# A fused attention and state-space kernel: its channel stage laid out with time on the rows and four channels a product

## The reference, cut to what matters

```python
x1  = x + attention(x)                  # out = o @ Wo.T + bo, o[b, c, 128]
y   = causal_conv(x1 * mask, taps[c])   # plus D[c] * x1, times mask again
W   = (unpacked_6_bit(qweight) - zero_point[n]) * scale[n]
out = x1 + y @ W.T + bias               # over time, for each b and c
```

## Time and profile before

| | us |
|---|---|
| median of 3 runs | 744.96 |
| lowest, highest | 742.61, 747.47 |
| the profiled execution, its own time | 743.27 |
| its span in the profile | 741.5 |
| busy: TensorE matmul, VectorE, ScalarE, GpSimd | 720.1, 610.1, 390.3, 215.9 |

### The profile page before, as it was taken

One profiled execution on the slowest core, in us unless ns is written; L12 is line 12 of the kernel. 1 busy time (PEld: TensorE's weight loads), 2 busy tenths in 40 slices (PEclk: granted clock), 3 DMA queues, 4 the chain that ended last, 5 costly groups with the idle time before them and its releaser, 6 DMA issues.

```text
span 741.5 us, 18118 instructions
## 1 busy us (share of the span) xinstructions
PE 720.1 (97%) x7540; PEld 595.0 (80%) x7540; DVE 610.1 (82%) x1085; ACT 390.3 (53%) x736; POOL 215.9 (29%) x224
## 2 busy tenths in 40 slices
PE   8999999999999999999999999999988899999996
PEld 6866878786978778697869787786766799999996
DVE  4878989998997977697767769777987688888887
ACT  4686475565656765746656565657552322333221
POOL 5370110030002011530300000000221778877772
PEclk9999999999999999999999999999999999999999
DMA  7800100020001001000200100022024288988861
GB/s 229 308 3 2 58 5 1 2 61 3 1 17 46 2 2 57 2 4 13 62 2 1 29 31 3 2 61 61 26 75 136 72 185 200 216 191 203 204 133 72
DMA packets 37108, 51.52 MB, mean 69 GB/s; under 512 B 7427, under 2 KB 23203, under 8 KB 36899
## 3 DMA queue, kind: packets, MB, share of 16 engines
q1 hardware_dynamic: 35042, 49.77, 25.7%
q0 software_dynamic: 1024, 0.53, 0.3%
q10 hardware_dynamic: 960, 0.06, 0.1%
HBM read 41.71 MB, written 8.63 MB: 68 GB/s over the span
## 4 chain that ended last, share of the span: by engine, by line
PE 88%; DVE 6%; ACT 2%; DMA 1%; issue 1%; SPq 0%; POOL 0%; DVEq 0%
PE ps L724 34%; PE ps L773 7%; PE ps L616 6%; PE ps L618 6%; PE ps L617 6%; PE ps L796 4%; PE ps L1052 4%; PE ps L1053 4%; PE ps L665 3%; PE ps L624 2%; PE ps L626 2%; PE ps L625 2%; PE ps L1021 2%; PE ps L1009 1%; PE ps L1011 1%
## 5 line engine op out<-in xcount | busy, mean ns | idle before, releaser
L1153 ACT ACTIVATE qt<-ps,m_bias 128x512 f32<-128x512 f32 x228 | 145.8, 685 | 89.3 <-PE ps L724 89.3
L724 PE MATMUL ps<-q_high,m_high 64*128 64x512 f32 x768 | 165.0, 397 | 0.0
L724 PE MATMUL ps<-q_high,m_low 64*128 64x512 f32 x768 | 161.3, 387 | 0.0
L724 PE MATMUL ps<-q_low,m_high 64*128 64x512 f32 x768 | 113.7, 387 | 0.0
L724 PEld LDWEIGHTS ps<-q_high,m_high 64*128 64x128 f32 x768 | 88.7, 184 | 14.8 <-issue 5.1
L724 PEld LDWEIGHTS ps<-q_high,m_low 64*128 64x128 f32 x768 | 88.8, 184 | 9.2
L1425 DVE TENSOR_TENSOR z_low<-ps,z_high 128x512 fp32r<-128x512 f32 x128 | 79.8, 683 | 19.7 <-ACT z_high L1173 19.7
L724 PEld LDWEIGHTS ps<-q_low,m_high 64*128 64x128 f32 x768 | 81.1, 184 | 10.2
L1173 ACT CAST z_high<-ps 128x512 fp32r<-128x512 f32 x128 | 66.7, 597 | 18.3 <-PE ps L840 9.2
L508 POOL TENSOR_TENSOR o_sum<-o_part,o_part 128x512 f32<-128x512 f32 x7 | 9.1, 1302 | 229.3 <-ACT o_part L1183 229.3
L1347 ACT COPY x1T_far<-ps 128x128 f32<-128x128 f32 x32 | 8.5, 265 | 103.8 <-PE ps L1021 103.8
(11 more groups left out here) (269 smaller groups left out, 1660.1 us busy)
## 6 DMA issues: line engine op xcount, KB each, us to landing
x_raw<-in_x_groups SPq DMA_DIRECT2D x32, 256.0 KB, 4.2
x_s<-in_x SPq DMA_DIRECT2D x32, 256.0 KB, 5.7
out<-res SPq DMA_DIRECT2D x31, 256.0 KB, 3.4
toep_high<-taps_scratch SPq DMA_DIRECT2D x32, 192.0 KB, 4.4
toep_low<-taps_scratch SPq DMA_DIRECT2D x32, 192.0 KB, 5.0
w_raw<-in_w_groups SPq DMA_DIRECT2D x8, 512.0 KB, 7.6
toep_far<-taps_scratch SPq DMA_DIRECT2D x32, 64.0 KB, 5.6
rope_raw<-in_rope_rows SPq DMA_DIRECT2D x8, 192.0 KB, 7.5
```

The costliest lines, as they stand in the source:

```text
L724: mm = pe.matmul(ps[:, fold_bank(u, j) + e, :], weights[rows, (GH * g + j) // 2, c, :], moving[c][rows, :], start=start, stop=stop)
L1153: act.activation(qt[:, j, :], ps[:, fold_bank(u, j) + j % 2, :], ACT.Identity, bias=m_bias[:, h:h + 1]).then_inc(s["qt_done"], 1)
```

## The change

The channel stage now has time on the rows throughout, and works on groups g of four channels.

- `attention_out(g, tt)` gives 128 times of four channels and 128 sequences (512 columns), with `Wo` stationary; five of them (`AHEAD`) are issued ahead of the first convolution. VectorE's `x1_made` adds `bo` (a column) and `x` in one instruction; ScalarE and VectorE split the result (`x1_rounded`, `x1_rest`). No transposes.
- `convolved(c)` reads one channel of the group's tiles. `through_ffn(g, n)` has the weights `wfT` stationary and makes 128 output times for the four channels, in 8 matmuls of 512 columns, one such product in each round.
- The sum of `y` over time is made by VectorE (`y_pair`), GpSimd (`y_sum`) and two matmuls with ones per group (`total`). ScalarE turns it into the correction with bias (`rest`), GpSimd adds `x1`, and VectorE scales the product and adds in one instruction.
- The weights come laid out by the host (`ffn_words`, `woT`, `x_channels`, the output likewise). `turned_ffn` and `turned_wo` are gone. VectorE masks bits in 4 instructions, ScalarE floats, GpSimd subtracts the zero row into `wfT` and makes `mask`, both during units 14 and 15. `woT_high` is made in unit 14 by ScalarE, `woT_low` ahead of `begun_last(0)` by VectorE, which also waits for `wfT` there. Five one-column VectorE instructions for the bit masks are new at the kernel's start.
- SP loads `x` in pieces of 1 MB per group, two before the stage; of the Toeplitz tiles only two channels' are issued at `t_ready` GH * NU, the other four behind `out_done`.

The diff, cut to its core: most removed lines are left out, since they stand in the listing above.

```diff
+    qw = t("qw", [P, TT, T], I32, at=wcT_at)
+    q_float = t("q_float", [P, TT, T], at=wcT_at)
...
+    wfT = t("wfT", [P, TT, T], F32R, at=m_at)
...
+    x_t = [t(f"x_t{n}", [P, TT, 4, B], at=at) for n, at in enumerate((m_at + 24 * KB, sc_at, qt_at, qt_at + 8 * KB))]
...
-    sp.wait_ge(s["feat_ready"], 4 * NS)
...
-        sp.dma_start(x_s[c][:], d["x"][:, c, :]).then_inc(ring_x[c], 16)
...
+    sp.dma_start(cols[:], d["columns"]).then_inc(s["cols_in"], 16)
+    sp.dma_start(z_row[:], d["zero_row"].partition_broadcast(P)).then_inc(s["row_in"], 16)
+    sp.dma_start(woT_raw[:], d["woT"]).then_inc(s["wo_in"], 16)
+    def load_x1(g):
+        sp.dma_start(x_t[g % RX][:], d["x_channels"][g]).then_inc(ring_x[g % RX], 16)
...
+    def store(i):
+        sp.wait_ge(s["res_done"], i + 1)
+        sp.dma_start(out[i // 4, :, i % 4], rest[i % RW][:]).then_inc(stored[i % RW], 16)
+    sp.wait_ge(s["t_ready"], GH * LAST)
+    load_x1(0)
+    sp.wait_ge(s["turn_done"], 4 * LAST)
+    load_x1(1)
+    sp.wait_ge(s["t_ready"], GH * NU)
+    sp.wait_ge(s["taps_stored"], 96)
+    for c in range(2):
         load_toep(c)
...
-            load_x1(c + RX - R)
...
+    sp.wait_ge(s["out_done"], NU)
+    for c in range(2, R):
         load_toep(c)
...
+    load_x1(2)
+    for c in range(C + 6):
+        if c == 4:
+            load_x1(3)
         if c + R < C:
...
+            sp.wait_ge(s["conv_ready"], c + 1)
+            load_toep(c + R)
+        if 0 <= c - 6:
+            store(c - 6)
+        if c >= 8 and c % 4 == 0 and c // 4 + 2 < NG:
+            sp.wait_ge(s["rest_ended"], c - 4)
+            load_x1(c // 4 + 2)
...
+    pool.wait_ge(s["row_in"], 16)
+    chain(pool.tensor_scalar(z_row[:], z_row[:], 0.0, 63.0, ALU.max, ALU.min))
+    chain(pool.tensor_scalar(z_row[:], z_row[:], MAGIC, None, ALU.add))
+    chain(pool.tensor_scalar(z_row[:], z_row[:], MAGIC, None, ALU.subtract))
+    pool.wait_ge(s["len_in"], 16)
+    chain(pool.tensor_copy(len_f[:], len_i[:]))
+    for k in range(TT):
+        pool.tensor_scalar(mask[:, k, :], len_f[:], l_pos[:, 0:1], float(P * k), ALU.subtract,
+                           ALU.is_gt).then_inc(s["mask_ready"], 1)
+        pool.wait_ge(s["mask_ready"], k + 1)
     pool.wait_ge(s["t_ready"], GH * LAST)
...
-    pool.tensor_tensor(c_row[:], c_row[:], s_row[:], ALU.mult).then_inc(s["c_done"], 1)
+    for k in range(TT):
+        pool.wait_ge(s["wf_ready"], k + 1)
+        pool.tensor_tensor(wfT[:, k, :], q_float[:, k, :], z_row[:], ALU.subtract).then_inc(s["wfT_done"], 1)
+        pool.wait_ge(s["wfT_done"], k + 1)
+    front(LAST - 1)
+    pool.memset(f(ones_r[:]), 1.0).then_inc(s["ones_ready"], 1)
...
-    def with_bo(c):
...
+    for c in range(C + 5):
+        i = c - 5
+        if i >= 0:
+            g, n = i // 4, i % 4
+            pool.wait_ge(s["rest_begun"], i + 1)
+            pool.tensor_tensor(rest[i % RW][:], rest[i % RW][:], x_t[g % RX][:, n], ALU.add).then_inc(s["rest_ended"], 1)
+        if c < C:
+            g, ch = c // 4, c % 4
+            pool.wait_ge(s["yh_done"], c + 1)
+            if g >= 2 and ch == 0:
+                pool.wait_ge(s["f_ready"], 4 * (g - 1))
+            pool.tensor_tensor(y_low[g % 2][:, :, ch, :], y[c % 2][:], f(y_high[g % 2][:, :, ch, :]),
+                               ALU.subtract).then_inc(s["yl_done"], 1)
+            pool.wait_ge(s["y_paired"], c + 1)
+            if g >= 1 and ch == 0:
+                pool.wait_ge(s["sum_low_done"], g)
+            pool.tensor_tensor(y_sum[:, ch, :], y_pair[c % 2][:, 0, :], y_pair[c % 2][:, 1, :],
+                               ALU.add).then_inc(s["y_summed"], 1)
...
-    def turned_ffn(k):
...
-            mm = pe.transpose(ps[:, FFN_BANK[k], n * P:(n + 1) * P], wf[n][:, k * P:(k + 1) * P], ident[:])
...
-    turned_wo()
...
-    pe.wait_ge(s["woT_done"], 1)
     kept_busy(BX, 4)
...
+    def attention_out(g, tt):
+        i = 4 * g + tt
+        if tt == 0:
+            pe.wait_ge(s["ol_done"], g + 1)
+        if i == 0:
             pe.wait_ge(s["ol_early"], 1)
...
             pe.wait_ge(s["woT_done"], 1)
             pe.wait_ge(s["zl_done"], 8 * NU)
...
-    def turned(c):
...
             pe.wait_ge(s["s_taken"], 4 * NU)
...
+        if i >= AHEAD:
+            pe.wait_ge(s["x1_done"], i - 1 if i >= AHEAD + 2 else i - AHEAD + 1)
+        part = slice(tt * P, (tt + 1) * P)
+        three(ps[:, a_bank(i), :], woT_high[:, part], woT_low[:, part], run_of(o_high[g % 2][:]),
+              run_of(o_low[g % 2][:])).then_inc(s["a_ready"], 1)
     def convolved(c):
...
+        g, ch, q = c // 4, c % 4, c % 2
+        if ch == 0:
+            pe.wait_ge(s["x1_low_done"], 4 * g + 4)
         pe.wait_ge(ring_toep[c % R], 48 * (c // R + 1))
         if c >= 2:
             pe.wait_ge(s["y_done"], c - 1)
         for e in range(TT - 1):
             rows = slice(e * P, (e + 1) * P)
...
+            three(ps[:, 4 + q, e * P:T].rearrange("p (t b) -> p t b", b=B), toep_high[c % R][:, rows],
+                  toep_low[c % R][:, rows], x1_high[g % 2][:, 0:TT - e, ch, :], x1_low[g % 2][:, 0:TT - e, ch, :],
+                  e == 0, False)
+        pe.matmul(ps[:, 4 + q, (TT - 1) * P:T], toep_far[c % R][:], x_t[g % RX][:, 0, ch, :], start=False,
+                  stop=True).then_inc(s["conv_ready"], 1)
+    def total(g):
+        pe.wait_ge(s["sum_low_done"], g + 1)
+        if g == 0:
+            pe.wait_ge(s["o_last"], 2)
+            pe.wait_ge(s["ones_ready"], 1)
         else:
...
+            pe.wait_ge(s["rest_begun"], 4 * g)
+        pe.matmul(ps[:, TOTAL_BANK, :], ones_r[:], run_of(sum_high[:]), start=True, stop=False)
+        pe.matmul(ps[:, TOTAL_BANK, :], ones_r[:], run_of(sum_low[:]), start=False, stop=True).then_inc(s["total_ready"], 1)
+    def through_ffn(g, n):
+        i = 4 * g + n
+        if n == 0:
+            pe.wait_ge(s["yh_done"], 4 * g + 4)
+        if i == 0:
+            pe.wait_ge(s["wfT_done"], TT)
+        if i < 3:
+            pe.wait_ge(s["x1_done"], i + 3)
+        else:
+            pe.wait_ge(s["res_done"], i - 2)
         for k in range(TT):
...
+            pe.matmul(ps[:, F_BANK[i % 3], :], wfT[:, k, n * P:(n + 1) * P], run_of(y_high[g % 2][:, k]), start=(k == 0),
+                      stop=False)
+        if n == 0:
+            pe.wait_ge(s["yl_done"], 4 * g + 4)
+        for k in range(TT):
+            mm = pe.matmul(ps[:, F_BANK[i % 3], :], wfT[:, k, n * P:(n + 1) * P], run_of(y_low[g % 2][:, k]), start=False,
+                           stop=(k == TT - 1))
         mm.then_inc(s["f_ready"], 1)
-    def projected_last():
...
+    for i in range(AHEAD):
+        attention_out(i // 4, i % 4)
+    for c in range(C):
+        g, ch = c // 4, c % 4
+        if c + AHEAD < C:
+            attention_out((c + AHEAD) // 4, (c + AHEAD) % 4)
+        if g >= 1 and ch == 1:
+            total(g - 1)
+        convolved(c)
+        if g >= 1:
+            through_ffn(g - 1, ch)
+    through_ffn(NG - 1, 0)
+    total(NG - 1)
+    for n in range(1, 4):
+        through_ffn(NG - 1, n)
...
+    def x1_rounded(i):
+        g, tt = i // 4, i % 4
+        act.wait_ge(s["x1_done"], i + 1)
+        if g >= 2 and tt == 0:
+            act.wait_ge(s["conv_ready"], 4 * (g - 1))
+        act.copy(x1_high[g % 2][:, tt], x_t[g % RX][:, tt]).then_inc(s["x1_high_done"], 1)
+    for i in range(TT):
+        x1_rounded(i)
+    split(1)
+    x1_rounded(TT)
+    for c in range(C + 5):
+        g, ch, i = c // 4, c % 4, c - 5
+        if ch == 0 and 1 <= g <= NG:
+            act.wait_ge(s["y_summed"], 4 * g)
+            if g >= 2:
+                act.wait_ge(s["total_ready"], g - 1)
+            act.copy(sum_high[:], y_sum[:]).then_inc(s["sum_high_done"], 1)
+        if ch == 1 and 2 <= g + 2 < NG:
+            split(g + 2)
+        if i >= 0:
+            act.wait_ge(s["total_ready"], i // 4 + 1)
+            act.wait_ge(s["z_scaled"], 1)
+            if i >= RW:
+                act.wait_ge(stored[i % RW], 16 * (i // RW))
+            act.activation(run_of(rest[i % RW][:]), ps[:, TOTAL_BANK, :], ACT.Identity, bias=fb_c[:, i % 4:i % 4 + 1],
+                           scale=z_scale[:, i % 4:i % 4 + 1]).then_inc(s["rest_begun"], 1)
+        if c + AHEAD < C:
+            x1_rounded(c + AHEAD)
+        if c < C:
+            act.wait_ge(s["y_done"], c + 1)
+            if g >= 2 and ch == 0:
+                act.wait_ge(s["f_ready"], 4 * (g - 1))
+            act.copy(y_high[g % 2][:, :, ch, :], y[c % 2][:]).then_inc(s["yh_done"], 1)
...
+    dve.wait_ge(s["woT_high_done"], 1)
+    dve.tensor_tensor(woT_low[:], woT_raw[:], f(woT_high[:]), ALU.subtract).then_inc(s["woT_done"], 1)
     begun_last(0)
...
+    def x1_made(i):
+        g, tt = i // 4, i % 4
+        dve.wait_ge(s["a_ready"], i + 1)
+        if tt == 0:
+            dve.wait_ge(ring_x[g % RX], 16 * (g // RX + 1))
+        if i == 0:
+            dve.wait_ge(s["cols_in"], 16)
+        x1 = run_of(x_t[g % RX][:, tt])
```

(42 more changed lines are left out.)

383 lines of the change are left out of this document (78 added, 305 removed).

## The result

The changed kernel takes 740.67 us (median of 9 runs, 738.13 to 742.93). The kernel before, run beside it, takes 744.96 (9 runs, 742.05 to 747.60). The ratio is 0.9943, with a 95% interval of 0.9921 to 0.9965: faster by 0.6%, or 4.3 us, where 10.0 was forecast. That lies within 1%, and inside the range. The sign was right, the size less than half of what was forecast. The profiled execution took 739.18 us, with a span of 737.3 us instead of 741.5, where 731.5 was forecast.

A forecast was written before the change was run, and what follows sets the result against it. TensorE was taken as the bound, VectorE and transfers not far behind. 714.5 to conv(31)'s end, 15.6 behind it and 1.2 for the clock gave 731.3; span taken as 731.5 (10.0 less), median 735.0, range 729.5 to 742.

The forecast's parts named there:

- first attention product: End of the attention: TensorE's first attention product of the channel stage at 572.1, 4.15 us earlier; bounds 0 and -4.4.
- conv(0) to the end of conv(31): Channel stage: convolutions, 26 attention and 27 linear products, `total` and 1.3 of waits sum to 133.4, ending at 714.5.
- Does something hide under that?: Channel stage: VectorE 3.6, GpSimd 3.0 and ScalarE below 2.5 fit in TensorE's mean round of 4.56; no transfer cost.
- Pause: End of the attention: TensorE's 3.22 us "issue" stop at 558.31, blamed on full transfer queues, goes; first attention product 4.15 earlier.
- pause stays: Rival, chance 0.15: the 3.22 us stop before the channel stage remains, 4.15 us are lost, time 739.2.
- Fill and clock: Start of the channel stage: TensorE idles 4.6 us, conv(0) starts at 581.1, lower clock adds 1.2 (ends 0 and +3.3).
- Steady rounds, plain ones: Channel stage: period of 4.45 without `total`, 0.46 more every fourth round, mean 4.56 instead of 4.86; strided operands cost 0.
- Tail: Behind conv(31): GpSimd's last four adds end at 11.3, then VectorE 0.755 and a store of 3.4: 15.6.
- The loop is not TensorE's: Rival, chance 0.09: VectorE or GpSimd waits for another engine each round, period stays 4.86, 8.4 us lost, time 743.4.
- Slower by repeated late instructions: Rival, chance 0.11: bunched 1 MB loads repeatedly delay TensorE's instruction blocks in the channel stage; 754.4 with four stops.

The follow-up runs named there:

- b2: b1 with GpSimd's `rest` in the round with `total` also waiting for `sum_low`; 734.91 us, 0.9884 of the kernel before.
- a1: Changed kernel with TensorE's `total` issued behind its round's convolution instead of ahead of it; 732.57 us, 0.9828 of the kernel before.
- b1: Changed kernel with GpSimd's `y_low` of a group's first channel waiting until VectorE's `sum_low` has ended; 737.04 us, 0.9889 of the kernel before.
- h1: Changed kernel with `total` behind the convolution, ScalarE's `split(1)` early, and VectorE's part of `split(1)` moved to GpSimd; 728.18 us, 0.9780 of the kernel before.
- e1: Kernel before with only two channels' Toeplitz tiles loaded ahead of `out_done`, the other four and the x rows behind it; 741.95 us, 0.9957 of the kernel before.
- d1: Changed kernel with all six channels' Toeplitz tiles loaded ahead of `out_done`, as in the kernel before; 740.53 us, 0.9942 of the kernel before.
- g1: d1 with 11 small float32 products, 22 matmuls whose results are overwritten, added ahead of `values(14,0)`; 744.23 us, 1.0010 of the kernel before.
- c1: Changed kernel with `split(1)` early: ahead of ScalarE's x1 roundings, behind VectorE's second `x1_made`; 738.23 us, 0.9901 of the kernel before.

## Why the prediction was right in sign and wrong in size

By its own steps, in the profiled execution:

| step | forecast | measured |
|---|---|---|
| first attention product | 572.1 | 573.32 |
| from there to conv(0), clock included | 10.2 | 9.45 |
| conv(0) to the end of conv(31) | 133.4 | 139.3 |
| behind conv(31) | 15.6 | 15.2 |
| span | 731.3 | 737.3 |

*The step that failed* is the one under "Does something hide under that?": "VectorE per round: ... a fourth each of split and `sum_low` 0.34: 3.6 of 4.56", and with it "the first `total` waits for VectorE's `sum_low` (+0.2). From then on VectorE waits for TensorE." It priced VectorE's new SBUF-to-SBUF instructions by rows in which GpSimd did not hold them up, and laid GpSimd's 3.0 us a round beside them as if the two had nothing in common. In the rounds with `total` two of them were stretched by 1.91 us in all. Of the seven totals ahead of conv(31) the first did not wait, and six waited 7.1 in all: +6.9 against the forecast's 0.2. `total` with its neighbours took 0.71 in those instead of 0.46: +1.5. conv(0) ran at the lower clock, 2.20 instead of 1.81, which the forecast had in another term: +0.4. Against that a plain round is shorter than forecast. By the starts from 650.31 to 654.65 it is 0.69 + 1.57 + 0.14 + 1.94 = 4.34: the plain-float32 tail takes 0.14 where 0.22 was read in the kernel before, and the linear layer 1.94 where 1.84 and 0.11 were forecast: 31 rounds, -3.4. Together +5.4 of the 5.9 between 133.4 and 139.3. The other 0.5 is not taken apart in full. Part of it lies in the first rounds: the forecast has 1.1 of waits there for low parts and `y_high`; the trace has one of 1.02, ahead of the ninth attention product, for `split(2)`, which VectorE made in 1.10 instead of 0.68 beside GpSimd's work. b2 shows the first term by taking its cause away, a1 by taking the wait away.

The trace of the kernel before held the warning, in rows that the forecast did not use. VectorE's form with two SBUF operands, L1606, takes 0.69 at 551.45 with GpSimd idle, and more beside GpSimd's work on `c_row`:

```profile
536.56 0.93 DVE L1606 TENSOR_TENSOR sc_last<-sc_last,row_stat 128x512 f32<-128x512 f32 x1
541.99 0.95 DVE L1606 TENSOR_TENSOR sc_last<-sc_last,row_stat 128x512 f32<-128x512 f32 x1
```

```profile
536.33 1.51 POOL L584 TENSOR_SCALAR c_row<-c_row 128x512 f32<-128x512 f32 x1
```

In its channel rounds only `o_low` (L1651) had two SBUF operands; it took 0.68 six times, and 1.35 once, at 578.55, so the kernel before hardly paid there. The change brought in two such instructions a round, `y_pair` and `x_low`, and `sum_low` in every fourth. The Trainium skill, "SBUF — State Buffer", section "Who interferes with whom", states that a VectorE instruction with two SBUF inputs contends with a GpSimd instruction that reads SBUF; its section "Summary: rules for kernel authors" adds that the second of the two to issue is blocked until the first has ended. By that rule `sum_low` ends about its own length behind `y_low`. The changed kernel's trace agrees, with 0.55 for an instruction of 0.69 and, behind `rest`, 0.29 for `y_pair`'s 0.42; b1 and b2 take the GpSimd instruction away, and the plain 0.68 and 0.42 are back. The first section's rule that a VectorE instruction with at most one SBUF input, outside the modes that use both ports, does not contend is borne out by h1's 2.82 us.

*Pause.* The size of the term was about right: A is 4.7 shorter, against a forecast of 4.15. The product itself came only 2.9 earlier, since what lies ahead of A had grown by 1.8. The cause given, that the paced loads remove the pause, was right in part, and that the term came out is partly luck. Pacing alone takes the pause of the kernel before from 3.22 to 0.75 (e1). But the change also takes instructions out of TensorE's stream, which moved the stop to another place, and there it is short even with the burst (d1, 0.40); g1 brings it back by moving the place. Either would have been enough. The rival "pause stays" fell for a reason that it did not name. The sentence of the Trainium skill that crossing a block's border is mostly hidden ("Runtime: NRT & Kernel Launch", "Instruction fetch mechanics") holds for most borders here, 57 packets with four "issue" waits of TensorE in the changed kernel's trace, and not for the one of 3.22 us. The product came 1.2 later than forecast: 0.6 was lost before unit 1, where "issue" waits of 0.33 and 0.98 stand at 21.80 and 32.42, and the rest mostly in VectorE's queue of units 14 and 15, where the last softmax transpose ended at 564.03 instead of 563.0.

*Fill and clock.* 3.85 us of idle instead of 4.6, the half clock as forecast: it cost 1.2 in the two products ahead of conv(0) and 0.4 in conv(0), against 1.2 in all. conv(0) began at 582.77 where 572.1 + 10.2 gave 582.3. c1 confirms the mechanism.

*Steady rounds, plain ones.* 4.34 instead of 4.45; the strided moving operands cost nothing, as taken.

*Tail.* 15.2 instead of 15.6. GpSimd's adds set the pace, as forecast: the last ends at 733.57, 11.5 behind the last convolution, where 11.3 was forecast. The span ends 2.9 behind the last VectorE instruction (734.36) instead of 3.4; 5.1 us from issue to landing is the median of all the stores, not what the last one took.

*Rivals.* "The loop is not TensorE's" named the right kind (VectorE waiting for GpSimd) and 743.4 for it; it looked for a wait by semaphore each round, where the trace has stretched instructions in one round of four. "Slower by repeated late instructions" did not occur.

## What to carry to other kernels

Before work is moved between VectorE and GpSimd, list for each VectorE instruction how many operands lie in SBUF. Those with two are priced with GpSimd's instruction added, where the two can meet; those with one in PSUM are not. If such an instruction feeds the bounding engine, let that engine ask for it later: here one moved call was worth 8.1 us, more than the whole change (4.3). A pause marked "issue" wants two things checked, how full the queues are and how fast the instructions ahead of it are used up; here 22 small matmuls some 17 us earlier moved it.

## What the runs showed of the hardware

- A VectorE instruction with two SBUF operands that starts behind a GpSimd instruction with SBUF operands is held until about that one's end: 0.69 became 1.76, 0.42 became 1.26. GpSimd is stretched the other way round, from 1.29 to 1.48 under `x_low`, and up to 1.77. With one operand in PSUM there was no such effect: four `x1_made` took 2.82 with GpSimd at work (h1) and without (the changed kernel).
- TensorE waited 2.90 us marked "issue" with 22 tiny matmuls added some 17 us earlier, and 0.40 without them, with the same transfers in flight.
- Idle stretches of TensorE of 3.85 and 2.85 us, and once 2.48 (g1, at 542.98), were followed by the lower clock level; those of 2.06 and once 2.90 were not. The rows do not tell why.
- Before unit 1, "issue" waits of 0.2 to 1.2 us stand between 19 and 33 us in twelve of the thirteen traces, with the 16 engines full there (1.03 from 20 to 30 us in the changed kernel). The kernel before has none in its trace, with 1.02. Their sum differs from trace to trace, up to 3.0 us in a1. How much of the spread of the runs they make is not shown, and pacing the loads there was not tried.
